# Attention units after the first layer: key products ahead of scores in one row strip, maxima in four parts, transposed maxima in another bank, one wait before the casts

## The reference, cut to what matters

```python
a = jax.nn.softmax(jnp.einsum('bhsd,bhtd->bhst', q, k) * D ** (-0.5), axis=-1)
if causal:
    mask = (jnp.arange(t)[None, :] > jnp.arange(s)[:, None]).astype(a.dtype)
    a = a * mask
o = jnp.einsum('bhst,bhtd->bhsd', a, v)
```

## Time and profile before

| | us |
|---|---|
| median of 3 runs | 1066.5 |
| the profiled execution, its own time | 1070.84 |
| its span, first to last instruction | 1069.0 |
| PE busy | 991.3 (93%) |
| DVE busy | 543.5 (51%) |
| ACT busy | 434.3 (41%) |
| POOL busy | 267.3 (25%) |
| mean granted TensorE clock | 0.986 |

### The profile page before, as it was taken

One profiled execution on the slowest core, in us unless ns is written; L12 is line 12 of the kernel. 1 busy time (PEld: TensorE's weight loads), 2 busy tenths in 40 slices (PEclk: granted clock), 3 DMA queues, 4 the chain that ended last, 5 costly groups with the idle time before them and its releaser, 6 DMA issues.

```text
span 1069.0 us, 20661 instructions
## 1 busy us (share of the span) xinstructions
PE 991.3 (93%) x8414; PEld 715.4 (67%) x8423; DVE 543.5 (51%) x1357; ACT 434.3 (41%) x635; POOL 267.3 (25%) x406
## 2 busy tenths in 40 slices
PE   6978777999999988999999999999999999999997
PEld 4656544555467766676676476776667768999996
DVE  5588789985359999831531335884133144100000
ACT  5666555676455555542312325553221221221220
POOL 3022201101124434432312111675121002332211
PEclk9999989999999999999999999999999999999999
DMA  9700000000050100000000020003312136755500
GB/s 259 96 2 2 2 1 0 2 1 0 1 116 4 42 2 3 3 1 1 1 0 1 1 98 2 3 2 118 120 39 90 42 120 231 274 187 200 171 28 1
DMA packets 55359, 60.55 MB, mean 57 GB/s; under 512 B 23603, under 2 KB 47071, under 8 KB 55266
## 3 DMA queue, kind: packets, MB, share of 16 engines
q1 hardware_dynamic: 52322, 52.93, 16.6%
q0 software_dynamic: 2944, 6.30, 1.8%
HBM read 54.76 MB, written 7.21 MB: 58 GB/s over the span
## 4 chain that ended last, share of the span: by engine, by line
PE 66%; DVE 17%; ACT 2%; issue 2%; POOL 1%; DMA 1%; DVEq 0%; POOLq 0%; ACTq 0%
PE ps L1957 15%; PE ps L2262 10%; PE ps L2406 8%; PE ps L2419 7%; DVE small L851 6%; PE ps L2083 3%; PE ps L2340 3%; PE ps L1833 2%; PE ps L1794 2%; PE ps L1791 2%; PE ps L1869 2%; PE ps L1732 2%; PE ps L2085 1%; DVE small L956 1%; PE ps L1826 1%
## 5 line engine op out<-in xcount | busy, mean ns | idle before, releaser
L851 DVE TENSOR_REDUCE small<-ps 128x2 f32<-128x512 f32 (+2 forms) x176 | 149.3, 901 | 52.2 <-PE ps L1794 35.3
L1957 PE MATMUL ps<-r_w,r_k 128*128 128x256 f32 x512 | 113.2, 381 | 2.5 <-ACT r_k L1630 2.5
L2262 PE MATMUL ps<-r_a,r_w 128*128 128x512 f32 x256 | 112.0, 594 | 3.1 <-ACT r_a L1462 3.1
L1957 PEld LDWEIGHTS ps<-r_w,r_k 128*128 128x128 f32 x512 | 96.4, 190 | 18.6 <-issue 4.4
L1388 ACT ACTIVATE r_a<-ps 120x1024 f32<-120x1024 f32 (+1 forms) x80 | 77.5, 1021 | 62.1 <-PE ps L1841 62.0
L2262 PEld LDWEIGHTS ps<-r_a,r_w 128*128 128x128 f32 x256 | 48.2, 190 | 59.8 <-issue 56.0
L2406 PE MATMUL ps<-r_a,w_block 128*128 128x128 f32 x736 | 86.4, 275 | 1.0 <-ACT r_a L1694 0.7
L2406 PEld LDWEIGHTS ps<-r_a,w_block 128*128 128x128 f32 x736 | 85.6, 192 | 2.5 <-ACT r_a L1694 1.0
L1630 ACT ACTIVATE r_k<-ps,pvec 128x512 f32<-128x512 f32 x64 | 44.0, 687 | 101.0 <-PE ps L2262 101.0
L2419 PE MATMUL ps<-w_all,r_a 128*128 x368 | 83.2, 379 | 0.2 <-issue 0.2
L1702 ACT ACTIVATE r_a<-ps 128x512 f32<-128x512 f32 x46 | 27.5, 597 | 129.0 <-PE ps L2406 119.9
(11 more groups left out here) (277 smaller groups left out, 1802.9 us busy)
## 6 DMA issues: line engine op xcount, KB each, us to landing
w_block<-in_L_ffn_W SPq DMA_DIRECT2D x23, 1024.0 KB
w_all<-in_L_ffn_W SPq DMA_DIRECT2D x8, 1024.0 KB, 10.2
r_w<-in_L_xattn_a_li_w SPq DMA_DIRECT2D x4, 1024.0 KB, 7.2
x_rows<-x_all SPq DMA_DIRECT2D x4, 512.0 KB, 3.0
x_rows<-r_a SPq DMA_DIRECT2D x4, 512.0 KB, 3.0
x_all<-in_x SPq DMA_DIRECT2D x3, 512.0 KB, 6.5
y_all<-in_L_ffn_w_gate SPq DMA_DIRECT2D x1, 1024.0 KB, 9.0
y_all<-in_L_ffn_w_up SPq DMA_DIRECT2D x1, 1024.0 KB, 11.4
```

The source lines that it names most:

```text
L851: ins_ = dve.tensor_reduce(nm.rearrange("p (j s) -> p j s", j=4)[:, j:j + count, :], src, AX.X, ALU.max, negate=True)
L1957: ins_ = pe.matmul(o[:, t // 2, (t % 2) * D:(t % 2 + 1) * D], src[:, c, t * P:(t + 1) * P], w[:, c, :], start=(c == 0), stop=(c == chunks ...
L2262: ins_ = pe.matmul(o, LI[a]["li2"][:, c, m * P:(m + 1) * P], FT3[:, c, :], start=(c == 0), stop=(c == KC - 1))
```

## The change

On VectorE: the maxima of an a1 or a2 unit are taken in four reduces of one bank each, in the order of banks 3, 0, 2, 1, where there were three (bank 3, bank 2, banks 0 and 1 together); the one of bank 0 waits for the second finished strip alone. The cast no longer waits for `half_max`, `value_max` and, in all but two units, `maxT_done`; one wait for VectorE's own last reduce is left. This last edit holds for L0 too. On TensorE: the transposed maxima of a1 and a2 go to bank 7 and no longer to bank 6, and in all iterations from the third on that still have scores to do (29 of a1's, 13 of a2's) `scores_and_keys` takes the place of `scores` and `keys_and_shifts`: in strip 2 both key products of unit n+1 stand first and the scores of n+2 after them, in strips 3, 0 and 1 the scores stand first and the key products after them.

```diff
-        def max_bank():
-            return key_bank(2)
+        def max_bank(n):
+            return key_bank(2 if UNIT_OF[n][0] == "L0" else 3)
...
-                    for j, count in ((2, 2), (0, 2)) if UNIT_OF[n][0] == "L0" else ((3, 1), (2, 1), (0, 2)):
-                        dve.wait_ge(sem["s_done"], 4 * n + (1 if j == 3 else 4))
+                    for j, count in ((2, 2), (0, 2)) if UNIT_OF[n][0] == "L0" else ((3, 1), (0, 1), (2, 1), (1, 1)):
+                        dve.wait_ge(sem["s_done"], 4 * n + {3: 1, 0: 2}.get(j, 4) if n >= L0_UNITS else 4 * n + 4)
...
-                    dve.wait_ge(sem["half_max"], n + 1)
-                    if n >= L0_UNITS:
-                        dve.wait_ge(sem["value_max"], n - L0_UNITS + 1)
                     step(ins_)
-                    if n >= 1:
+                    if n in (FIRST["a1"] + 2, FIRST["a2"] + 2):
                         dve.wait_ge(sem["maxT_done"], n)
...
+                def scores_and_keys(n):
+
+                    first = n < FIRST[UNIT_OF[n][0]] + 3
+                    key_scores(n - 1, (2,), 0)
+                    if not first:
+                        pe.wait_ge(sem["sums_read"], n - 2)
+                    scores_of(n, (3, 0, 1), 0)
+                    key_scores(n - 1, (2,), 1)
+                    scores_of(n, (3, 0, 1), 1)
+                    if not first:
+                        pe.wait_ge(sem["os_ready"], n - 2 - L0_UNITS)
+                    scores_of(n, (2,), 0)
+                    pe.wait_ge(sem["maxT_ready"], n)
+                    key_scores(n - 1, (3,), 0)
+                    pe.wait_ge(sem["exp_done"], 2 * (n - 1))
+                    key_scores(n - 1, (0, 1), 0)
+                    scores_of(n, (2,), 1)
+                    key_scores(n - 1, (3, 0, 1), 1)
+                    shifts(n - 1)
...
-                        if n + 2 < n1 and not begun and not third:
+                        mixed = a != "L0" and n + 2 < n1 and n > n0
+                        if mixed:
+                            scores_and_keys(n + 2)
+                        elif n + 2 < n1 and not begun and not third:
                             scores(n + 2)
...
-                        if n + 1 < n1:
+                        if n + 1 < n1 and not mixed:
                             keys_and_shifts(n + 1)
```

More of the change, by code:

```diff
@@ L1379, in max_copy @@
                     act.wait_ge(sem["maxT_done"], n + 1)
-                    act.activation(maxT[:], max_bank()[:, 0:S], ACT.Copy).then_inc(sem["maxT_ready"], 1)
+                    act.activation(maxT[:], max_bank(n)[:, 0:S], ACT.Copy).then_inc(sem["maxT_ready"], 1)
                 def exponentials(n):
@@ L1825, in max_transposes @@
                     for t in range(T):
-                        ins_ = pe.transpose(max_bank()[:, t * P:(t + 1) * P], MX[:, t, :], ident[:])
+                        ins_ = pe.transpose(max_bank(n)[:, t * P:(t + 1) * P], MX[:, t, :], ident[:])
                     ins_.then_inc(sem["maxT_done"], 1)
```

## The result

The kernel after takes 1061.3 us (median of 5 runs, 1060.9 to 1062.1) against 1066.6 us before (1066.0 to 1067.1): ratio 0.995, 95% interval 0.9937 to 0.9964. Run again beside other kernels it gave 0.9927 (0.9913 to 0.9941). So it is 5 to 8 us faster. 1056.8 was forecast, with 1053.5 to 1063.5 as the range: the direction and the range hold. The gain is 5.2 and 8.2 us in the two comparisons, where the sum had 9.7, and 1061.3 lies just outside the forecast's own range, 1054 to 1061; it is inside only the range that was widened to take in rival A.

What follows compares the result with a forecast made beforehand. VectorE was taken to bound a1, TensorE a2 (strip 2 starting late), and a ring of both L0. Terms 0.5 + 2.5 + 1.6 + 5.1 = 9.7 us off 1066.5 gave 1056.8 us, range 1053.5 to 1063.5.

Steps and rivals of the forecast that it cites:

- the forecast's own range: Whole kernel: 1054 to 1061 us, from gains of 12.5 down to 5.5 off 1066.5.
- rival A: Whole kernel: gain stops at the next wait, a2's order brings 0.1 a unit, masks move to L908; 1062.4 us, chance 0.17.
- L0, casts: L0: idle time ahead of the cast falls from 0.09 to 0.04 in 10 units, 0.5 us (bounds 0 and 0.8).
- a1, 28 periods: a1: VectorE's period falls from 4.59 to 4.50, 2.5 us, and slow casts beside masks go, 1.6 us.
- The casts' waits: VectorE, a1 and a2: with one wait the cast's 0.20 gap falls to 0.04, 0.16 less per unit.
- rival C: a1 and a2: the cast's 0.20 is not due to its waits and stays; 1.5 us gained, 1065.0, chance 0.08.
- Four reduces: VectorE: four reduces instead of three cost 0.07 more per unit in a1, 0.08 in a2 (bounds 0.05 and 0.15).
- a1's masks: a1, units with statistics: later values keep GpSimd's masks off the casts, 4 x 0.4 = 1.6 us (bounds nothing and 2.0).
- The order in a2: TensorE, a2: strip 2 starts on time with key products first; period 4.89 to 4.50, 5.1 us (bounds 2.0 and 5.8).
- three rings (TensorE, VectorE, bank 2's values): a2: periods of 4.40 or 4.47 for TensorE, 4.44 for VectorE, values' ring within 0.1; 4.50 taken.
- Rival B: TensorE, a1 and a2: changing between key products and scores costs time; 1070.6 us at 0.1 a change, chance 0.07.
- The difference of the profiled executions: Whole kernel: before's profiled execution lies 4.3 us above the median of runs, and this difference was carried over.

Runs made afterwards that it cites:

- 10: The kernel before, unchanged, profiled once more: 1066.0 us, span 1064.1.
- 9: One wait ahead of all casts; a1 with order, bank and three reduces of before, a2 as in after: 1059.2 us, ratio 0.9932 to before.
- experiment 11: The kernel after without the fourth mask block of each a1 unit: 1057.1 us in one run.
- experiment 6: The kernel before with only the four reduces of one bank in a1 and a2: 1066.8 us, ratio 1.0 to before.
- experiment 2: The kernel after with scores and key products in the order of before, keeping four reduces, one cast wait and bank 7: 1062.9 us, ratio 0.9956 to before.
- experiment 5: The kernel before with three of the cast's four waits taken out: 1061.8 us, ratio 0.9954 to before.
- experiment 7: The kernel after with VectorE transposing only half of the sums in a2, the other half left out of the output: 1059.4 us, ratio 0.9929 to before.
- experiment 8: The kernel after with the reduces in the order 3, 2, 0, 1: 1066.3 us, ratio 0.9993 to before.

## Why the prediction was right or wrong

| step | forecast | measured |
|---|---|---|
| L0, casts | 0.5 us | 0.6 at a granted clock of 1.00 |
| a1, 28 periods | 2.5 + 1.6 = 4.1 | 3.3 |
| a2, 13 periods | 5.1 | 2.2 |
| sum | 9.7 | 6.1 |

The measured sum lies between the two comparisons in time (5.2 and 8.2 us). L0's 0.6 is not from after: its 15 periods take 72.2 in 10 and 71.6 in 9 and 11, all three at 1.00. At 0.96 they take 74.3 in before and 6, and 73.3 to 73.8 in after, 2, 5 and 7, so 0.5 to 1.0 less. The clock moves this stretch by more than the edit does.

**The casts' waits: the gap was right, its worth in part by luck.** The gap went from 0.20 to 0.03 in every unit, so rival C, that it isn't the waits', is out. Experiment 5 gives 134.8 - 130.6 = 4.2 in a1, where 28 x 0.16 = 4.5 was the term, but not in the way I had it. The first 13 periods give 1.1, not 2.1: plain ones only 0.03 each, since the second ring holds them at 4.56, and 0.7 of the 1.1 is one place where before takes 4.66, 5.09 and 4.74 in a row, with 0.55 ahead of a cast. The 11 periods with statistics and between them give 2.6, not 1.8, since the slow casts go as well. The same 0.7 is in the change's 3.3. By the Trainium skill, page "VectorE: DVE Perf Modes", section "The DRAIN you can't avoid", a semaphore after each of a row of VectorE operations costs nothing extra. That is one semaphore an operation. It does not carry over to four waits ahead of one: they cost 0.17 us more than one wait, and they cost it where wait instructions stand behind the wait for the last reduce.

**Four reduces: right in size.** 0.07 in a1 (4.59 to 4.66, experiment 6). No cast of 0.43 is left; but experiment 5 has none with three reduces, so the casts' waits alone do this too, and the 1.6 us are not the later values' alone.

**a1's masks: the bound came true, not the value.** I took the whole 1.6 us, with "if the masks now disturb the product on L908" as the lower bound. They do: the later values start the masks between the casts and the product's end, and in 14 units the product takes 0.65. Experiment 11 (one run) removes that and 1.6 us. In plain units, which I had left out of this step, it costs 0.07 of period in every second one (4.58 beside 4.51); of the rest, 0.08 had been idle time ahead of the reduces, and by 0.07 they now start before the product ends (337.11 against 336.53 + 0.65). By the Trainium skill, page "SBUF — State Buffer", section "Who interferes with whom", a VectorE instruction with two SBUF inputs contends with a GpSimd instruction that reads SBUF, and the ports they share are an exclusive lock. The trace agrees: L905 has two such inputs and got 0.23 us longer, within the length of one of the four selects (1.48 / 4 = 0.37).

**The order in a2: this step failed.** Its term was 13 x 0.39 = 5.1 us and measured 2.2, for want of the wait for `sums_read`. "The block from scores to sums falls from 2.65 to between 2.16 and 2.23" came near (2.29), but the scores begin 0.18 later than I put them. I had checked three rings (TensorE, VectorE, bank 2's values) and not the one through bank 3: low part, transposition of the sums 0.10 + 0.71, scores 0.05, first reduce 678.63 - 677.38 = 1.25, and 681.23 - 678.63 = 2.60 to the next low part; 4.71. Before, this ring stood at 4.89 beside the one through ScalarE's copy: in experiment 2 the scores begin 0.97 after the low part, 0.11 later than `sums_read` alone would have them (0.10 + 0.71 + 0.05), and the period is 4.89 still. I took away the second and left the first. Experiment 7 shortens one member by 0.27 and the period falls by 0.18, to where TensorE's transposes and the first key product are what the scores follow; 4.53 is close to the 4.50 that I had taken for the rings I had. Of 2.9 us missing here, 2.1 are this wait. Of the rest, 0.3 is the long first period, which I had counted as a thirteenth steady one, and about 12 x 0.03 that the period is then 4.53 and not 4.50.

**Rival A** had the right outcome for the total, for a mechanism of its kind (the gain stops at the next wait), but at a wait that it didn't name: neither the value ring nor the copied maxima. Its other half, masks that move from the casts to L908, came true in 14 units. I had given it 0.17 and the forecast 0.68, and the total came out nearer to it (1062.4) in the first comparison; that it lies in my range owes more to the width of the range than to the sum for a2. The forecast's range itself was not built from its own bounds: masks entered with 0.5 where I had written nothing, a2 with 13 x 0.28 where I had written 13 x 0.15, and with the written ones it would have ended at 1063.1.

**Rival B is out as a price of changing.** Six changes leave a1's block at 2.54 us. But "slower" was nearer than my 0.07 for it: the order alone is 7.5 us slower, through bank 2's late scores and the reduce that stands second for them. I had written that in a1 the order changes nothing that counts. That holds only because the same change puts bank 0 second and bank 2 third (experiment 8); I had costed the new order of the reduces as a loss of slack and not seen what it protects from.

**The difference of the profiled executions** was carried over as 4.3 us above the median, which was right for before. After's profile lies 0.4 under its median, so a comparison of the two spans shows 9.9 and would have seemed to confirm the sum. It was the second profile of before that showed otherwise.

What stays open: what the 0.35 us are by which the cast of a1's thirteenth unit is late in both profiles of before (the trace has them between the two wait instructions), and why a1 with three reduces and the old order keeps 4.56 in its early units and 4.43 in later ones, after a unit with statistics has been between. A transposition of the sums in two pieces, which would let strip 3's first half go early with nothing left out, wasn't tried, since TensorE would then write a bank that VectorE reads.

## What to carry to other kernels

When a wait on a ring goes, list every semaphore that stands in the same program stretch, early ones too, and work out each one's ring to its end: the one that was hidden is the next limit. An order of producers and an order of consumers are one edit: each of the two alone was worth nothing or a loss here, while the wait list of a short instruction was worth 5 us by itself. Look at what stands behind a wait for an engine's own last instruction: further waits that were long met still have to be gone through there. And profile the old kernel twice before you read a difference of spans.

## What the runs showed of the hardware that I had not expected

- Waits have a price of their own on VectorE, though all but the one for its own last reduce were long met: 0.20 us ahead of the cast with four waits, 0.09 with three (L0), 0.03 with one. It is not a price per wait: the casts with two waits in after (the third unit of a1 and of a2) have 0.03 as well, since the second wait instruction runs ahead of the last reduce's end.
- Masks on GpSimd lengthen a 128x256 product on VectorE from 0.42 to 0.65 (experiment 11 shows it). Where a mask block starts at a cast of 128x8, this takes up to 0.43 and not 0.17, and the small subtraction behind it between 0.28 and 0.38; that is read from their meeting in time.
- Row strips do not keep the program's order among each other: in before key products start at 706.04, ahead of a score product at 706.31 that stands before them in the program. Products of other shapes (32*120 and 32*128) start within 0.01 us of each other (677.69 and 677.70 in experiment 7).
